# Gathered streams in a graph kernel: five loops of indirect DMAs that may not run more than a set number of columns ahead of their consumers

## The chip, the cores and the metric

The kernel runs on one core of a Trainium2 chip. A core has TensorE (PE), VectorE (DVE), ScalarE (ACT), GpSimd (POOL) and SyncE (SP), each with its own instruction stream; they meet through semaphores, and 16 DMA engines move data for them. The metric is the device time of one execution in microseconds (us), lower is better.

## The reference, cut to what matters

Four graph layers follow each other on 100000 nodes of 16 features and 50000 edges sorted by destination. Each layer normalizes the nodes, gathers a row of the source node for every edge, makes a message of it and sums the messages by destination:

```python
h = jnp.maximum(_layernorm(x, axis=-1), 0.0)
x = x + _L0_gnn_ref(h, edge_index, ...)   # attention, 3 heads, then 1 head: h[src] * alpha, twice
h = jnp.maximum(_layernorm(x, axis=-1), 0.0)
x = x + _L1_gnn_ref(h, edge_index, edge_type_8, ...)   # two passes: x[src] @ W[relation], mean by relation
h = jnp.maximum(_layernorm(x, axis=-1), 0.0)
x = x + _L2_gnn_ref(h, src, dst, edge_weight)          # messages summed at the source
h = jnp.maximum(_layernorm(x, axis=-1), 0.0)
x = x + _L3_gnn_ref(h, edge_attr_16, ..., src, dst, edge_type_90)   # h[src] @ W_rel[type] * e
```

## The kernel before

**Layout.** The edges are laid out as 128 partitions by T = 392 columns. A column of a gather is one indirect DMA that GpSimd issues: 128 rows of a table in DRAM, one to each partition, at indices from `src_i` or `idx2`. The program runs in stages; all engines meet at a barrier between two stages (L131, L132). In each stage every engine has one instruction stream, written out by the loops of its block, and the code's order is the order on the engine.

**The five gather streams that the change touches**, in the order of the program:

| stage | gathers (line before) | columns | consumer, unit | the use that is counted |
|---|---|---|---|---|
| first, attention layer 1 (`g1`) | `ring<-t_gat,src_i` L1147 | 56 to 391 (EARLY = 56 are gathered a section earlier) | VectorE, 48 columns, reads at L1271 | `mix_ok`, by `g_mix` L1362 |
| second, attention layer 2 (`g2`) | `g_ring<-t_gat,idx` L1487 | 0 to 391 | VectorE, 40 columns, L1617 | `ring_free`, by `g_S` L1637 |
| third, relation pass 1 (`r1`) | `r_ring<-t_rel,idx` L1817 | 0 to 391 | VectorE, 8 columns, L2010 | `expand_ok`, by L2010 |
| fourth, relation pass 2 (`r2`) | `r_ring<-t_rel,idx` L2128 | 0 to 391 | TensorE, 8 columns, L2160 | before `lift_ok` (L2160); in the change `taken`, after VectorE's reduce L2243 |
| last, layer 4 (`l3`) | `l_ring<-t_last,idx` L2573 | 0 to 391 | VectorE, 8 columns, L2655 | `mats_used`, after L2660 |

**What paces them.** A batch is eight columns with a landing semaphore `gat_in[n]` of its own. `paced` (L61 to L67) is asked before every gather; at each eighth column it waits for a landing: below column 160 (RUN) for that of the batch before the last, from 160 on for that of the batch just issued:

```python
    n = s // BATCH - (1 if s >= RUN else 2)
    if s % BATCH == 0 and n >= first // BATCH:
        engine.wait_ge(landing[n], 16 * BATCH)
```

`hold` is a plain `wait_ge`. In the second stage it keeps GpSimd from writing over a ring of 200 columns (NR = 5 blocks of QN = 40) that is still in use, at columns 200, 240, 280, 320 and 360; in the fourth, with 240 columns, at 240, 280, 320 and 360. In the third the ring has all columns and the hold is never reached. The consumers wait for their columns' landings with `all_landed` (L78 to L81).

After the gathers of the last stage GpSimd writes the result by columns into `fin` (L2583, 393 indirect DMAs, waits of `spaced` on L75 and of `final_ok`), and SyncE copies `fin` to the output. Two other streams of indirect DMAs stay as they are: the payload gathers of the first section (L521, landing waits on L520) and the scatter-adds between the fourth and the last stage (L2352, waits on L2351).

Of the kernel before, what the change touches and what calls it, by code (L numbers as in the profile page):

```python
# [69 lines left out]
def spaced(engine, landing, s):  # L70


    n = s // BATCH - 2
    if n >= 0:
        engine.wait_ge(landing[n], 16 * BATCH)  # L75


# [10 lines left out]
def gnn_kernel(nc, x, src, dst, edge_attr_16, edge_type_8, edge_type_90, edge_weight,  # L88
# [45 lines left out]
    with ExitStack() as top:  # L134
# [954 lines left out]
        with ExitStack() as ctx:  # L1089
# [52 lines left out]
            with nc.Block() as block:  # L1142
                @block.gpsimd
                def _(pool):
                    for s in range(EARLY, T):
                        paced(pool, gat_in, s, EARLY)
                        pool.indirect_dma_start(ring1[:, s, :], None, t_gat1,  # L1147
                                                bass.IndirectOffsetOnAxis(src_i[:, s:s + 1], 0)
                                                ).then_inc(gat_in[s // BATCH], 16)
                    all_landed(pool, gat_in, EARLY, T)  # L1150
# [270 lines left out]
        with ExitStack() as ctx:  # L1421
# [58 lines left out]
            with nc.Block() as block:  # L1480
                @block.gpsimd
                def _(pool):
                    for s in range(T):
                        if s % QN == 0 and s >= NR * QN:
                            hold(pool, ring_free, s // QN - NR + 1)
                        paced(pool, gat_in, s)
                        pool.indirect_dma_start(ring[:, s % (NR * QN), :], None, t_gat2,  # L1487
                                                bass.IndirectOffsetOnAxis(idx2[:, s:s + 1], 0)
                                                ).then_inc(gat_in[s // BATCH], 16)
# [272 lines left out]
        def relation_pass(tag, table, table_out, F, CW, weights, root, bias, NR, norm, setup):  # L1762
# [13 lines left out]
            with ExitStack() as ctx:  # L1776
# [32 lines left out]
                with nc.Block() as block:  # L1809
                    @block.gpsimd  # L1810
                    def _(pool):
                        for s in range(T):
                            if s % QN == 0 and s >= NR * QN:
                                i = s // QN - NR
                                hold(pool, expand_ok, first[i] + subs[i])
                            paced(pool, gat_in, s)
# [269 lines left out]
        with ExitStack() as ctx:  # L2086
# [33 lines left out]
            with nc.Block() as block:  # L2120
                @block.gpsimd
                def _(pool):
                    for s in range(T):
                        if s % QN == 0 and s >= NR * QN:
                            i = s // QN - NR
                            hold(pool, lift_ok, first[i] + subs[i])
                        paced(pool, gat_in, s)
# [411 lines left out]
        with ExitStack() as ctx:  # L2539
# [28 lines left out]
            with nc.Block() as block:  # L2568
                @block.gpsimd
                def _(pool):  # L2570
                    for s in range(T):
                        paced(pool, gat_in, s)
                        pool.indirect_dma_start(ring[:, s, :], None, t_last,  # L2573
# [133 lines left out]
```

## Time and profile before

| | us |
|---|---|
| median of 3 runs | 6640.55 |
| lowest, highest | 6635.97, 6644.13 |
| span of the profiled execution | 6645.3 |
| GpSimd busy in the span | 4320.0 (65%) |
| VectorE busy | 3659.5 (55%) |
| TensorE busy | 2965.9 (45%) |
| ScalarE busy | 1167.0 (18%) |

The profiled execution's time is 6645.3 us, of which its span is all, 4.8 us over the median of the runs. The rows below come from it. A row of a group of instructions gives their number, their busy time and mean duration, and the idle time of the engine just before them with what ended it; "issue" is idle time in which the engine waited for nothing that the profile shows. A landing wait shows as a wait for the DMA. EVENT_SEMAPHORE is an instruction that only waits for semaphores or sets them; POOLq is GpSimd's sequencer, which runs it. The chain of work that ended last consists of the writes to `fin` on GpSimd.

### The profile page before, as it was taken

How to read it: one execution, taken by the hardware profiler on the slowest of the kernel's cores; microseconds unless marked ns; L12 is line 12 of the kernel's file. 1: busy time of each engine (PE TensorE's matmuls, PEld its weight loads, DVE VectorE, ACT ScalarE, POOL GpSimd, SP SyncE). 2: the span in 40 equal slices, each digit the busy share in tenths (PEclk: the TensorE clock that was granted, in tenths of full speed). 3: DMA queues.
4: the chain of work that ended last, by engine and by line, in shares of the span. 5: the costliest groups of instructions: out<-in, count | busy, mean ns of one | idle time of the engine just before them, and what ended most of it. 6: DMA issues, size and time to landing. Idle time of an engine off the chain costs nothing. (4 is left out here: it accounts for less than half of the span.)

```text
span 6645.3 us, 44822 instructions
## 1 busy us (share of the span) xinstructions
PE 2965.9 (45%) x13056; PEld 2260.1 (34%) x13056; DVE 3659.5 (55%) x8917; ACT 1167.0 (18%) x1912; POOL 4320.0 (65%) x3949
## 2 busy tenths in 40 slices
PE   5798699974444344447655443111111002544000
PEld 2477555543333233346644333111111001433000
DVE  8855499976555566654347667433322068876000
ACT  0265454532222233211111100000000000000000
POOL 4666555557762776376657665888888823766776
PEclk9899899985666555556667665555555555776555
DMA  2122222221110322123222212222222234211001
GB/s 41 22 62 70 56 67 67 66 66 12 20 17 14 89 60 65 47 64 100 84 87 60 64 53 72 52 36 36 44 27 27 5 96 154 57 50 37 7 7 44
DMA packets 283354, 350.11 MB, mean 53 GB/s; under 512 B 133518, under 2 KB 204432, under 8 KB 281970
## 3 DMA queue, kind: packets, MB, share of 16 engines
q1 hardware_dynamic: 112158, 295.24, 13.2%
q0 software_dynamic: 169376, 41.40, 7.8%
q10 hardware_dynamic: 1576, 10.60, 0.7%
q8 instruction: 105, 1.72, 0.1%
q14 instruction: 139, 1.14, 0.1%
HBM read 231.06 MB, written 122.29 MB: 53 GB/s over the span
## 5 line engine op out<-in xcount | busy, mean ns | idle before, releaser
L2352 POOL DMA_INDIRECT acc<-l_rows,l_uniq x392 | 624.1, 1592 | 121.0 <-issue 108.6
L2573 POOL DMA_INDIRECT l_ring<-t_last,idx x392 | 392.4, 1001 | 366.5 <-ACTq L2568 207.6
L521 POOL DMA_INDIRECT pay<-in_x,gidx x392 | 460.1, 1174 | 235.4 <-DMA pay<-in_x,gidx 114.3
L2393 PE MATMUL ps_l<-l_msg,l_alike 128*128 128x16 f32 x784 | 176.3, 376 | 962.4 <-DVE l_msg L2456 962.4
L1487 POOL DMA_INDIRECT g_ring<-t_gat,idx x392 | 416.1, 1062 | 278.7 <-issue 110.1
L1817 POOL DMA_INDIRECT r_ring<-t_rel,idx x392 | 414.6, 1058 | 254.6 <-issue 110.3
L809 POOL DMA_INDIRECT t_sort<-pay,c_pos x392 | 384.8, 982 | 296.3 <-DVE c_pos L875 196.3
L901 PE MATMUL ps_c<-plane,c_hit 128*128 128x400 f32 x1568 | 542.6, 499 | 1.2 <-ACT c_hit L827 1.2
L2128 POOL DMA_INDIRECT r_ring<-t_rel,idx x392 | 392.7, 1002 | 224.4 <-issue 110.4
L2338 POOL DMA_INDIRECT l_ring<-t_mix,idx x392 | 426.3, 1087 | 154.6 <-issue 119.1
L2393 PEld LDWEIGHTS ps_l<-l_msg,l_alike 128*128 128x128 f32 x784 | 171.0, 331 | 967.7 <-DVE l_msg L2456 967.7
L1147 POOL DMA_INDIRECT ring<-t_gat,src_i x336 | 368.5, 1097 | 151.5 <-issue 93.3
L2583 POOL DMA_INDIRECT fin<-X,home_i x393 | 376.9, 959 | 119.8 <-issue 119.8
L2614 PE MATMUL ps_l<-w_rel,l_pick 128*128 128x256 f32 x784 | 275.7, 528 | 272.7 <-DVE l_pick L2643 272.7
L901 PEld LDWEIGHTS ps_c<-plane,c_hit 128*128 128x128 f32 x1568 | 296.4, 190 | 208.3 <-ACT c_hit L827 1.6
L2614 PEld LDWEIGHTS ps_l<-w_rel,l_pick 128*128 128x128 f32 x784 | 212.0, 277 | 336.1 <-DVE l_pick L2643 291.6
L2451 DVE TENSOR_SCALAR l_den<-l_ring 128x128 f32<-128x128 f32 x49 | 11.2, 228 | 564.3 <-DMA l_ring<-t_mix,idx 564.3
L871 DVE SCALAR_TENSOR_TENSOR c_junk<-iota_lo,lo_f,ps_c 128x400 f32<-128x400 f16 x392 | 231.0, 623 | 63.1 <-PE ps_c L901 63.0
L688 PE MATMUL ps_a<-w_ext,a_act_t 96*128 96x128 f32 x1600 | 224.5, 286 | 40.4 <-DVE a_row L612 39.9
L688 PEld LDWEIGHTS ps_a<-w_ext,a_act_t 96*128 96x128 f32 x1600 | 214.8, 200 | 61.7 <-DVE a_row L612 49.8
L1520 PE MATMUL ps_g<-ident,g_ex 128*128 128x128 f32 x300 | 71.9, 426 | 327.0 <-DVE g_ex L1704 327.0
L622 DVE SCALAR_TENSOR_TENSOR a_act_t<-a_ex,a_pos 96x512 f32<-96x512 f32 x200 | 137.4, 687 | 143.5 <-ACT a_ex L729 140.1
(529 smaller groups left out, 8145.0 us busy)
## 6 DMA issues: line engine op xcount, KB each, us to landing
c_rows_d<-row_dst SPq DMA_DIRECT2D x98, 256.0 KB, 3.3
l_keys<-row_at SPq DMA_DIRECT2D x49, 512.0 KB, 4.2
l_typs<-row_typ SPq DMA_DIRECT2D x49, 512.0 KB, 3.7
g_hs<-t_gat SPq DMA_DIRECT2D x30, 660.0 KB, 4.7
acc<-r_zero SPq DMA_DIRECT2D x60, 320.0 KB
t_rel<-r_row SPq DMA_DIRECT2D x30, 640.0 KB, 3.5
r_hs<-t_rel SPq DMA_DIRECT2D x30, 640.0 KB, 4.7
d_gain<-acc SPq DMA_DIRECT2D x30, 640.0 KB, 6.0
```

The costliest lines, as they stand in the source:

```text
L521: pool.indirect_dma_start(pay[:, s, 8:PAY], None, x, bass.IndirectOffsetOnAxis(gidx[:, s:s + 1], 0)).then_inc(gat_in[s // BATCH], 16)
L688: last = mm(ps[:, at:at + WIDE], act_t[:, u, P * m:P * (m + 1)], w2_ext[:], start=True, stop=True, skip_group_check=True)
L809: pool.indirect_dma_start(t_sort, bass.IndirectOffsetOnAxis(pos[:, e:e + 1], 0), pay[:, e, :], None).then_inc(sent, 16)
L901: last = mm(ps[:, bank:bank + LO], hit[:, b, j, P * s:P * (s + 1)], plane[:, b, LO * j:LO * (j + 1)], start=(j == 0), stop=(j == 1))
L1487: pool.indirect_dma_start(ring[:, s % (NR * QN), :], None, t_gat2, bass.IndirectOffsetOnAxis(idx2[:, s:s + 1], 0)).then_inc(gat_in[s // BA ...
L1817: pool.indirect_dma_start(ring[:, s % (NR * QN), :], None, table, bass.IndirectOffsetOnAxis(idx2[:, s:s + 1], 0)).then_inc(gat_in[s // BAT ...
L2128: pool.indirect_dma_start(ring[:, s % (NR * QN), :], None, t_rel2, bass.IndirectOffsetOnAxis(idx2[:, s:s + 1], 0)).then_inc(gat_in[s // BA ...
L2338: pool.indirect_dma_start(ring[:, s, :], None, t_mix, bass.IndirectOffsetOnAxis(idx2[:, s:s + 1], 0)).then_inc(gat_in[s // BATCH], 16)
L2352: pool.indirect_dma_start(acc[r], bass.IndirectOffsetOnAxis(uniq[:, s:s + 1], 0), rows[:, (s // ES) % RR, s % ES, :], None, compute_op=ALU.add
L2573: pool.indirect_dma_start(ring[:, s, :], None, t_last, bass.IndirectOffsetOnAxis(idx2[:, s:s + 1], 0)).then_inc(gat_in[s // BATCH], 16)
L2583: pool.indirect_dma_start(fin, bass.IndirectOffsetOnAxis(home_i[:, s:s + 1], 0), X[:, s, :], None).then_inc(sent[s // BATCH], 16)
L2614: last = mm(ps[:, at:at + 256], pick[:, e % 2, s], w_rel[:].rearrange("p i o -> p (i o)"), start=True, stop=True)
```

## The change

A helper `credit` is added and called before `paced` in the five gather loops; the two kinds of `hold` go. At every eighth column past `lead` it waits until the consumers have reported the use of all but the last `lead` columns: `lead` is 96 (2 * EW), 64, 64, 32 and 40. In the fourth stage the count is now `taken`, which VectorE raises after its reduce, in place of `lift_ok`.

```diff
--- before.py
+++ after.py
@@ -73,6 +73,12 @@
     n = s // BATCH - 2
     if n >= 0:
         engine.wait_ge(landing[n], 16 * BATCH)
+
+
+def credit(engine, used, s, lead, per):
+
+    if s % BATCH == 0 and s > lead:
+        engine.wait_ge(used, -(-(s - lead) // per))
 
 
 def all_landed(engine, landing, lo, hi):
@@ -1143,6 +1149,7 @@
                 @block.gpsimd
                 def _(pool):
                     for s in range(EARLY, T):
+                        credit(pool, mix_ok, s, 2 * EW, EW)
                         paced(pool, gat_in, s, EARLY)
                         pool.indirect_dma_start(ring1[:, s, :], None, t_gat1,
                                                 bass.IndirectOffsetOnAxis(src_i[:, s:s + 1], 0)
@@ -1481,8 +1488,7 @@
                 @block.gpsimd
                 def _(pool):
                     for s in range(T):
-                        if s % QN == 0 and s >= NR * QN:
-                            hold(pool, ring_free, s // QN - NR + 1)
+                        credit(pool, ring_free, s, 64, QN)
                         paced(pool, gat_in, s)
                         pool.indirect_dma_start(ring[:, s % (NR * QN), :], None, t_gat2,
                                                 bass.IndirectOffsetOnAxis(idx2[:, s:s + 1], 0)
@@ -1810,9 +1816,7 @@
                     @block.gpsimd
                     def _(pool):
                         for s in range(T):
-                            if s % QN == 0 and s >= NR * QN:
-                                i = s // QN - NR
-                                hold(pool, expand_ok, first[i] + subs[i])
+                            credit(pool, expand_ok, s, 64, ES)
                             paced(pool, gat_in, s)
                             pool.indirect_dma_start(ring[:, s % (NR * QN), :], None, table,
                                                     bass.IndirectOffsetOnAxis(idx2[:, s:s + 1], 0)
@@ -2121,9 +2125,7 @@
                 @block.gpsimd
                 def _(pool):
                     for s in range(T):
-                        if s % QN == 0 and s >= NR * QN:
-                            i = s // QN - NR
-                            hold(pool, lift_ok, first[i] + subs[i])
+                        credit(pool, taken, s, 32, ES)
                         paced(pool, gat_in, s)
                         pool.indirect_dma_start(ring[:, s % (NR * QN), :], None, t_rel2,
                                                 bass.IndirectOffsetOnAxis(idx2[:, s:s + 1], 0)
@@ -2569,6 +2571,7 @@
                 @block.gpsimd
                 def _(pool):
                     for s in range(T):
+                        credit(pool, mats_used, s, 40, ES)
                         paced(pool, gat_in, s)
                         pool.indirect_dma_start(ring[:, s, :], None, t_last,
                                                 bass.IndirectOffsetOnAxis(idx2[:, s:s + 1], 0)
```

GpSimd's instructions stand in the same order in both kernels, and those of the other engines are unchanged. What differs is the waits. In the rows below a name in brackets is a semaphore that the DMA, or an instruction just ahead of it, waits for. Semaphores are used again from stage to stage and are printed by the first name that each had: every name but the last one of a pair (`a_down`, `a_row2`, `s_rows` and so on) is the landing semaphore of an earlier batch of this stage.

GpSimd in the second stage, columns 184 to 200, before:

```order
L1487 DMA g_ring<-t_gat,idx 128x33 [waits a_down]
L1487 DMA g_ring<-t_gat,idx 128x33 x7
L1487 DMA g_ring<-t_gat,idx 128x33 [waits a_row2]
L1487 DMA g_ring<-t_gat,idx 128x33 x7
L1487 DMA g_ring<-t_gat,idx 128x33 [waits a_out2_0,g2_ring_free]
```

and with the change:

```order
L1493 DMA g_ring<-t_gat,idx 128x33 [waits a_down,g2_ring_free]
L1493 DMA g_ring<-t_gat,idx 128x33 x7
L1493 DMA g_ring<-t_gat,idx 128x33 [waits a_row2,g2_ring_free]
L1493 DMA g_ring<-t_gat,idx 128x33 x7
L1493 DMA g_ring<-t_gat,idx 128x33 [waits a_out2_0,g2_ring_free]
```

Column 200 has its two waits in both; columns 184 and 192, and every eighth column from 72 on, have a second one only now.

GpSimd at the end of the last stage's gathers, columns 376 to 391, and the first writes to `fin`, before:

```order
L2573 DMA l_ring<-t_last,idx 128x16 [waits a_gat_in20]
L2573 DMA l_ring<-t_last,idx 128x16 x7
L2573 DMA l_ring<-t_last,idx 128x16 [waits a_gat_in21]
L2573 DMA l_ring<-t_last,idx 128x16 x7
L2583 DMA fin<-X,home_i 152704x16 [waits a_gat_in32,a_gat_in34]
L2583 DMA fin<-X,home_i 152704x16 x15
```

and with the change (`a_gat_in29` stands for `mats_used`):

```order
L2576 DMA l_ring<-t_last,idx 128x16 [waits a_gat_in20,a_gat_in29]
L2576 DMA l_ring<-t_last,idx 128x16 x7
L2576 DMA l_ring<-t_last,idx 128x16 [waits a_gat_in21,a_gat_in29]
L2576 DMA l_ring<-t_last,idx 128x16 x7
L2586 DMA fin<-X,home_i 152704x16 [waits a_gat_in32,a_gat_in34]
L2586 DMA fin<-X,home_i 152704x16 x15
```

The gathers have a second wait from column 48 on; the writes to `fin` have what they had.

## Rows read from the trace of the kernel before

**Rows 1.** Groups by line, GpSimd: xcount | busy, mean ns | idle before <-releasers

```profile
L1147 POOL DMA_INDIRECT ring<-t_gat,src_i x336 | 368.5, 1097 | 151.5 <-issue 93.3 <-DMA ring<-t_gat,src_i 50.4 <-POOLq L132 7.8
L1487 POOL DMA_INDIRECT g_ring<-t_gat,idx x392 | 416.1, 1062 | 278.7 <-issue 110.1 <-POOLq L132 109.3 <-DMA g_ring<-t_gat,idx 59.3
L1817 POOL DMA_INDIRECT r_ring<-t_rel,idx x392 | 414.6, 1058 | 254.6 <-issue 110.3 <-POOLq L132 76.2 <-DMA r_ring<-t_rel,idx 68.1
L2128 POOL DMA_INDIRECT r_ring<-t_rel,idx x392 | 392.7, 1002 | 224.4 <-issue 110.4 <-DMA r_ring<-t_rel,idx 71.3 <-POOLq L132 34.4
L2573 POOL DMA_INDIRECT l_ring<-t_last,idx x392 | 392.4, 1001 | 366.5 <-ACTq L2568 207.6 <-issue 110.0 <-DMA l_ring<-t_last,idx 48.9
```

**Rows 2.** Waits of the consumers for gathers: us in total, times, longest us

```profile
DVE idx L1271 <- DMA ring<-t_gat,src_i: 71.5, 7, 13.9
DVE g_score L1617 <- DMA g_ring<-t_gat,idx: 108.6, 10, 35.7
DVE r_msg L2010 <- DMA r_ring<-t_rel,idx: 58.0, 7, 9.7
PE r_ps L2160 <- DMA r_ring<-t_rel,idx: 284.1, 49, 9.3
DVE l_pick L2643 <- DMA l_ring<-t_last,idx: 98.3, 32, 4.1
```

**Rows 3.** Timeline, stage ends: start us, us, engine line op [idle before <-releaser]

```profile
2047.54 0.21 DVE L1271 CAST idx<-ring 128x48 int32<-128x48 f32 x1 [12.76 <-DMA ring<-t_gat,src_i]
...
2753.66 0.21 DVE L1617 TENSOR_TENSOR g_score<-g_ring,g_ad_slot 128x32 f32<-128x32 f32 x1 [0.61 <-DMA g_ring<-t_gat,idx]
...
3410.62 1.23 DVE L2010 TENSOR_TENSOR r_msg<-r_ring,r_hot 128x1024 f32<-128x1024 f32 x1 [8.56 <-DMA r_ring<-t_rel,idx]
...
4041.33 0.48 PE L2160 MATMUL r_ps<-ident,r_ring 128*128 128x128 f32 x1 [3.62 <-DMA r_ring<-t_rel,idx]
...
6123.73 0.98 POOL L2583 DMA_INDIRECT fin<-X,home_i  x1 [0.30 <-issue]
```

**Rows 4.** Instructions up to a credit: count, ns min/median/max, first and last start us

```profile
L1487 POOL DMA_INDIRECT g_ring<-t_gat,idx x153: 938/944/2504, 2166.7 to 2377.6; - x153
L1637 DVE TENSOR_TENSOR g_S<-g_ring,ps_g x3: 1486/1486/1486, 2225.6 to 2347.0; 128x1280 f32<-128x1280 f32 x3
L2128 POOL DMA_INDIRECT r_ring<-t_rel,idx x49: 940/944/1274, 3455.8 to 3515.7; - x49
L2243 DVE TENSOR_REDUCE r_Y<-r_chosen x4: 1004/1006/1007, 3470.8 to 3489.9; 128x64 f32<-128x512 f32 x4
```

**Rows 5.** Semaphore instructions by line: count, ns min/median/max, first and last start us

```profile
L67 POOLq EVENT_SEMAPHORE  x9: 17/17/17, 2450.8 to 3988.2; - x9
L520 POOLq EVENT_SEMAPHORE  x35: 17/17/17, 82.8 to 739.2; - x35
L75 POOLq EVENT_SEMAPHORE  x10: 17/17/17, 6165.6 to 6610.0; - x10
L2351 POOLq EVENT_SEMAPHORE  x48: 42/43/43, 4220.0 to 5349.3; - x48
```

**Rows 6.** Timeline, second stage, GpSimd: columns 192, 200, 312 and 320

```profile
2439.47 0.94 POOL L1487 DMA_INDIRECT g_ring<-t_gat,idx  x1 [1.75 <-DMA g_ring<-t_gat,idx]
...
2451.54 0.94 POOL L1487 DMA_INDIRECT g_ring<-t_gat,idx  x1 [2.21 <-DMA g_ring<-t_gat,idx]
...
2626.70 0.94 POOL L1487 DMA_INDIRECT g_ring<-t_gat,idx  x1 [1.76 <-DMA g_ring<-t_gat,idx]
...
2638.71 0.95 POOL L1487 DMA_INDIRECT g_ring<-t_gat,idx  x1 [2.15 <-DMA g_ring<-t_gat,idx]
```

**Rows 7.** Timeline, first section, GpSimd: two landing waits of L521

```profile
253.57 1.50 POOL L521 DMA_INDIRECT pay<-in_x,gidx  x1 [2.19 <-DMA pay<-in_x,gidx]
...
282.07 2.42 POOL L521 DMA_INDIRECT pay<-in_x,gidx  x1 [1.69 <-DMA pay<-in_x,gidx]
```

**Rows 8.** GpSimd before the writes to fin: us in total, times, longest us

```profile
POOL fin L2583 <- issue: 119.8, 393, 0.3
```

## The prediction

> **What bounds the kernel now.** First the list of GpSimd's groups [rows 1]. Five stages that the change touches gather 336 to 392 columns each (one indirect DMA per column, 128 rows), and they look alike: a gather is busy for about 1.0 to 1.1 us, 0.3 us of "issue" lies before each, and once in eight, from column 160 on, the engine waits for its own landings. Per stage that is 25 to 30 such waits of 49 to 71 us in all [rows 1]. (The fourth's other four are the ones with the old hold.) Busy, issue and landing waits of the second stage are 416.1 + 110.1 + 59.3 = 585.5 us, and from its first gather's start, 2166.7, to its last one's end, 2751.3 + 0.9, pass 585.5 us. So GpSimd does nothing else and never waits for a consumer.
>
> Next, who waits for the gathers [rows 2]: the consumers do, in every stage: VectorE 10 times in the second, 7 times in the first and third, 32 times in the last; TensorE 49 times in the fourth. The last such waits stand at the end of their stages [rows 3]: column 336 of the first is awaited for 12.76 us, column 360 of the second for 0.61, column 376 of the third for 8.56, column 384 of the fourth for 3.62. In the last stage the column writes to `fin` follow the last gather on the same engine after 0.30 us, and the program's end is GpSimd's chain of these writes. Every one of the five gather streams therefore sets its stage's end: what a batch of eight costs more, the program pays.
>
> **Part 1, the credits as waits.** The credit holds a gather until the consumers have used all but 96, 64, 64, 32 or 40 columns. Would it ever hold? I laid each of the 203 credits against the use that it asks for. The smallest reserve is in the fourth stage, with its lead of 32: column 48, the 49th gather, starts at 3515.7, and its credit asks for the fourth reduce, L2243, which ends at 3489.9 + 1.0 = 3490.9, 25 us earlier. In the second stage it is column 152, the 153rd gather, at 2377.6; the third `g_S` product ends at 2347.0 + 1.5 = 2348.5, 29 us earlier [rows 4]. The other three stages have no less. The consumers wait for gathers, so they are never 32 to 96 columns behind. The credits hold nothing, no gather starts later by them, and nothing is gained from pacing: **0 us**. The same shows that the two old holds, at nine places, held nothing, so that taking them away gives no time either.
>
> **Part 2, the credits as instructions.** An instruction on GpSimd carries one wait of its own kind; a second one goes into a semaphore instruction ahead of it. The built order shows it: in the kernel before, the gathers of these stages have one wait each but for nine (five in the second stage, four in the fourth, where the old hold stood); in the changed one, 36 + 40 + 40 + 44 + 43 = 203 have two. So 194 semaphore instructions come in, and it is the landing wait that moves into them, since the credit, asked first in the code, stays on the DMA. The trace has these nine, all on L67 [rows 5]. Their own duration is 17 ns. What the move costs is seen from the gather after:
>
> With a semaphore instruction, column 200 starts after 2.21 us of idle time, column 320 after 2.15; without, columns 192 and 312, the batches before, after 1.75 and 1.76 [rows 6]. The differences are 0.46 and 0.39 us. The semaphore instruction of column 200 stands at 2450.8 [rows 5], when the landing is seen, and the gather starts at 2451.54, 0.7 us later. The payload gathers of the first section, L521, tell the same: of their 48 landing waits 35 stand on an instruction of their own [rows 5], for instance the one of 2.19 us, and 13 on the DMA, as the one of 1.69 [rows 7]: 0.50 apart. Behind the semaphore instruction on GpSimd are queued the gather itself and the seven of its batch, all of them later by this much. I take **0.48 us** for a landing wait that the engine really sits out, between the 0.46 of column 200 and the 0.50 of L521, where both kinds are many. The ends are the smallest difference, 0.39, and 2.21 - 1.69 = 0.52, across the two streams.
>
> [...]
>
> Where the landing came long before, the instruction is free. Below column 160 `paced` asks for the batch before the last. The 10 semaphore instructions on L75, for the writes to `fin`, are of that kind, and all 393 writes start 0.3 us after the one before [rows 5, 8]. So 58 of the 203 credits, those below column 160 (7, 11, 11, 15 and 14), cost 0.
>
> From column 160 on there are 29 landing waits per stage. In the first the one of column 384 comes after the last gather that anyone waits for, so 28; in the second 29 - 5 = 24 and in the fourth 29 - 4 = 25 are new; the third and the last have 29 each. Sum: 28 + 24 + 29 + 25 + 29 = 135, times 0.48 = **65 us**. By stage 13.4, 11.5, 13.9, 12.0 and 13.9. Nothing hides it: the engines that could are waiting for these very landings [rows 2, 3]. In the third stage VectorE has the columns up to about 264 in hand before it needs them, but the sum of the delays arrives at columns 272 to 376, where it waits. The second is bound by least, 0.61 us, yet VectorE is in it because of nine earlier waits of the same kind, 108.6 us with it [rows 2], and they slip too.
>
> The section with the scatter-adds and those before it keep their order and their time. So the profiled span goes from 6645.3 to 6645.3 + 65 = 6710. The median of the runs shown, 6640.55, is 4.8 us less than that span; against it the sum is 6640.55 + 65 = **6705 us**.
>
> **A term that I don't take.** Gathers last 1.00 to 1.10 us on average where the shortest and the median are 0.94 (the median stands in [rows 4]): over the 1904 gathers of [rows 1], busy for 1984.3 us, 1984.3 - 1904 x 0.944 = 187 us of stretch, in some of them, while VectorE and the other engines work. Spread over 3% more time it might shrink by as much, 6 us; or not. I keep it for the low end.
>
> **The rivals.**
> Costs more than it pays: mine, at 6705.
> (a) Not slower: the semaphore instruction costs only itself. All 194 at 17 to 43 ns [rows 5] are 3 to 8 us, which gives 6644 to 6649, within 0.2%. For it speaks that every instruction on L75 is hidden; against it, that the nine of exactly the kind in question are not. It decides at whether the landing is already there when the sequencer arrives: from column 160 on it is not. A page of the Trainium skill would price it so too (Advanced Engine Details and Errata, Network/Comms): reading a semaphore from a sequencer takes 50 to 100 ns, by which 135 would be an estimated 7 to 14 us; the nine rows of this trace say more.
> (b) Only the last stage pays, because the others find slack behind their last gathers: 6640.55 + 29 x 0.48 = 6654. Against it stand the waits of [rows 3].
> (c) The credits do hold. In the fourth stage the reserve is 25 us; if consumers that start late by 12 us lost that reserve (they would have to fall behind the gathers, not with them), each of the stage's ten slots could add some 1 to 3 us: 6715 to 6735.
> (d) Faster: gathers spread thinner leave VectorE undisturbed and the stretch of 187 us falls by 65 + 13 us, some 40%. As the distance between gathers and consumers does not change, I see nothing that would do it: 6627.
>
> **How the numbers follow.** Mine has 0.86, (a) 0.06, (b) 0.03, (c) 0.03, (d) 0.02. Mine alone spans 135 x 0.39 = 53 to 135 x 0.52 = 70 us: 6693 to 6711. Less the 6 us of stretch it begins at 6687, taken as 6686; landings in the third and fourth stage that collide otherwise than before (their landing waits vary most, 68.1 and 71.3 us in all [rows 1]) may add 7 us at the other end: 6718. That range, 6686 to 6718, holds about 0.8 of the chance; (a), (b) and (d) stay outside. 0.2% is 13 us, about what a measurement of this kernel can tell from no change. Faster by more: 0.02; within: (a) and half of (b), 0.07; slower by more: 0.91.
>
> **What would show it.** Right: 203 semaphore instructions on the landing wait's line in the changed trace; from column 160 on landing waits of 2.1 to 2.2 us where 1.6 to 1.8 stood, and each stage's gather stream longer by 11.5 to 14; the gathers below column 160 at 0.30 us as before; no wait of GpSimd put down to VectorE or to the credit. The third and the fifth stage begin 25 and 51 us later than before. Wrong would be: unchanged landing waits (then a), GpSimd waiting for `g_mix`, `r_Y` or `l_wide` (then c), a mean gather under 1.0 us (then d), or longer streams with stage ends that don't move (then b).

## The result, and the profile after

The changed kernel takes **6687.57 us** (median of 4 runs, 6681.19 to 6690.97) beside 6642.34 us for the kernel before on the same chip: ratio 1.007, 95% interval 1.0056 to 1.0085. It is 45 us slower; 65 were forecast, and the time lies 1.6 us above the low end of the range (6686). Its profiled span is 6679.1 us beside 6645.3. The two medians are 45 us apart and the two profiled spans 34, because the profile of before is one of its slower executions and the profile of after one of its faster ones; stage by stage I compare profiles, the total by medians.

That is one chip. Chips are not alike for this program: the experiments ran in three groups, each on one chip with the kernel before beside it, which took 6641.03, 7803.52 and 7782.79 us in them. On the last of these chips the same changed kernel was **10.8% faster** than before (below). The prediction speaks of the chip that its profile came from.

GpSimd's groups by line in the changed kernel, as in [rows 1] (xcount | busy, mean ns | idle before, releasers):

```profile
L1154 POOL DMA_INDIRECT ring<-t_gat,src_i x336 | 370.0, 1101 | 164.1 <-issue 91.4 <-DMA ring<-t_gat,src_i 58.2 <-POOLq L138 7.8
L1493 POOL DMA_INDIRECT g_ring<-t_gat,idx x392 | 416.7, 1063 | 288.4 <-POOLq L138 108.8 <-issue 107.9 <-DMA g_ring<-t_gat,idx 62.2
L1821 POOL DMA_INDIRECT r_ring<-t_rel,idx x392 | 409.0, 1043 | 257.4 <-issue 107.0 <-POOLq L138 76.3 <-DMA r_ring<-t_rel,idx 74.2
L2130 POOL DMA_INDIRECT r_ring<-t_rel,idx x392 | 388.9, 992 | 241.9 <-issue 111.2 <-DMA r_ring<-t_rel,idx 95.1 <-POOLq L138 35.6
L2576 POOL DMA_INDIRECT l_ring<-t_last,idx x392 | 380.4, 970 | 380.3 <-ACTq L2570 207.5 <-issue 106.0 <-DMA l_ring<-t_last,idx 66.7
```

Against [rows 1] the idle time grew by 12.6, 9.7, 2.8, 17.5 and 13.8 us, in all 56.4, and the busy time changed by +1.5, +0.6, -5.6, -3.8 and -12.0, in all -19.3. The three largest releasers of a group stand in these lines. The list of all waits of GpSimd has two more, which are put down to VectorE, the sign by which a credit that holds was to be known (us in total, times, longest us):

```profile
POOL g_ring L1493 <- DVE g_S L1643: 9.5, 4, 2.9
...
POOL ring L1154 <- DVE g_mix L1369: 6.6, 3, 2.2
```

They are landing waits as long as their neighbours. The operation named merely ended at about the time of the landing; the one that the gather's credit asks for had ended at least 55 us before the gather started. I laid all 203 credits of the changed trace against the use that they ask for, as the prediction did for the trace before: the smallest reserve is 24.8 us, again at column 48 of the fourth stage (where a use is four columns). So on this chip no credit held GpSimd.

The semaphore instructions of L67, as [rows 5] has them (count, ns min/median/max, first and last start), and behind them columns 192, 200 and 312 of the second stage, as in [rows 6] (start us, us, [idle before]).

```profile
L67 POOLq EVENT_SEMAPHORE  x203: 17/17/17, 1602.0 to 6147.1; - x102
```

The timeline of those columns:

```profile
2455.12 0.95 POOL L1493 DMA_INDIRECT g_ring<-t_gat,idx  x1 [2.18 <-DMA g_ring<-t_gat,idx]
...
2467.02 0.95 POOL L1493 DMA_INDIRECT g_ring<-t_gat,idx  x1 [2.21 <-DMA g_ring<-t_gat,idx]
...
2647.82 1.35 POOL L1493 DMA_INDIRECT g_ring<-t_gat,idx  x1 [2.30 <-DMA g_ring<-t_gat,idx]
```

Nine became 203. Column 200, which had its semaphore instruction before, waits 2.21 us as it did; columns 192 and 312, which had none, went from 1.75 and 1.76 us to 2.18 and 2.30.

Who waits for the gathers (as [rows 2]: us in total, times, longest us):

```profile
DVE g_score L1623 <- DMA g_ring<-t_gat,idx: 119.0, 10, 34.8
DVE l_pick L2646 <- DMA l_ring<-t_last,idx: 99.5, 31, 4.1
DVE idx L1278 <- DMA ring<-t_gat,src_i: 83.2, 7, 15.8
DVE r_msg L2014 <- DMA r_ring<-t_rel,idx: 52.2, 6, 9.8
PE r_ps L2162 <- DMA r_ring<-t_rel,idx: 297.9, 49, 9.3
```

The last such waits of the stages, and between them the third stage's first gather, behind them the first write to `fin` (timeline, as [rows 3]):

```profile
2059.32 0.20 DVE L1278 CAST idx<-ring 128x48 int32<-128x48 f32 x1 [15.83 <-DMA ring<-t_gat,src_i]
...
2776.78 0.21 DVE L1623 TENSOR_TENSOR g_score<-g_ring,g_ad_slot 128x32 f32<-128x32 f32 x1 [0.72 <-DMA g_ring<-t_gat,idx]
...
2851.53 0.94 POOL L1821 DMA_INDIRECT r_ring<-t_rel,idx  x1 [76.28 <-POOLq L138]
...
3430.89 1.23 DVE L2014 TENSOR_TENSOR r_msg<-r_ring,r_hot 128x1024 f32<-128x1024 f32 x1 [9.75 <-DMA r_ring<-t_rel,idx]
...
4061.46 0.47 PE L2162 MATMUL r_ps<-ident,r_ring 128*128 128x128 f32 x1 [8.79 <-DMA r_ring<-t_rel,idx]
...
6157.86 0.99 POOL L2586 DMA_INDIRECT fin<-X,home_i  x1 [0.30 <-issue]
```

The same consumers wait as before, and longer, but for `r_msg` of the third stage, whose stream did not grow. The second stage's last awaited column comes 23.1 us later than in [rows 3] and the first write to `fin` 34.1 us later, so the program pays what the streams pay. The third stage begins at 2851.5, 23 us later (25 were forecast); the last at 5604.4 instead of 5572.1, 32 us later (51 were forecast). The shortfall lies in the third and the last stream: the fourth's 582.8 us became 595.2, as forecast, the third's 593.0 became 590.1 and the last's 551.3 became 553.2.

### The profile page after: what moved, and what is told of

Read it like the earlier page. It is cut to its first block and busy times, and to the rows that moved or that the text cites. A ratio compares the mean times of both kernels' runs of the same rounds, so it can differ in the third digit from the quotient of the medians.

```text
span 6679.1 us, 45016 instructions
## 1 busy us (share of the span) xinstructions
PE 2967.6 (44%) x13056; PEld 2261.4 (34%) x13056; DVE 3659.5 (55%) x8917; ACT 1168.3 (17%) x1912; POOL 4299.8 (64%) x3949
```

## The experiments

Stream lengths are from a stream's first gather's start to its last one's end. First four kernels on one chip (kernel before: 6641.03 us, 23 runs).

**1. The credit on the semaphore instruction, the landing wait on the DMA.** All five loops of the changed kernel, with two lines swapped:

```diff
-                        credit(pool, mix_ok, s, 2 * EW, EW)
                         paced(pool, gat_in, s, EARLY)
+                        credit(pool, mix_ok, s, 2 * EW, EW)
```

> The changed kernel with the two waits in the other order in the code (landing wait first, credit second), so that the landing wait stays on the gather itself and the credit goes into the semaphore instruction. All 203 credits are still asked. Theory A (the 45 us come from landing waits that stand on a semaphore instruction): the time of the kernel before, 6642 us, ratio 1.000; landing waits of the second stage back at 1.7 to 1.8 us from 2.2. Rival B (keeping GpSimd within 32 to 96 columns costs or moves something by itself): about that of the changed kernel, 6688, ratio 1.007.

Measured: 6628.27 us, ratio 0.9985 (0.9976 to 0.9993). The same 203 credits, the same 194 added instructions, now for the credit (count, ns min/median/max, first and last start), and the loss is gone:

```profile
L81 POOLq EVENT_SEMAPHORE  x203: 17/17/17, 1597.1 to 6077.2; - x102
```

L81 is the wait in `credit`. Beyond that, 13 us are gained. The nine old landing waits now stand on their DMAs too, which at 0.48 us each would be 4.3, but by the streams they are worth more: the second and fourth are 11.7 and 6.5 us shorter than before (table below; 9.3 and 6.3 in experiment 3, where only those nine differ in them). The second stage shows how. Before, column 200's gather starts at 2451.54 [rows 6] and column 216's here:

```profile
2477.91 1.54 POOL L1487 DMA_INDIRECT g_ring<-t_gat,idx  x1 [1.76 <-DMA g_ring<-t_gat,idx]
```

In experiment 1 the same two:

```profile
2451.67 0.94 POOL L1493 DMA_INDIRECT g_ring<-t_gat,idx  x1 [1.77 <-DMA g_ring<-t_gat,idx]
...
2475.99 0.94 POOL L1493 DMA_INDIRECT g_ring<-t_gat,idx  x1 [1.73 <-DMA g_ring<-t_gat,idx]
```

The landing wait of column 200 is 0.44 us shorter, and behind it the sixteen gathers take 24.32 us where they took 26.37. The waits between them are alike; the gathers last less, since three of them took over 2 us before and one does now. So a batch that starts 0.44 us later can also bring its gathers to places where they last longer, and this one wait was worth 2.5 us. So neither the credits as waits nor the instructions' own time cost anything that can be seen here; rival (a)'s "costs only itself" is true of an instruction whose wait is met, and only of that.

**2. The second wait alone.** The kernel before, its old holds kept, with a wait for a landing two batches older than the one that `paced` asks for from column 160 on, met long before, at the places of the credits:

```diff
+def older(engine, landing, s, lead):
+    n = s // BATCH - 3
+    if s % BATCH == 0 and s > lead:
+        engine.wait_ge(landing[n], 16 * BATCH)
...
+                        older(pool, gat_in, s, 64)
```

> The kernel before, no credits, old holds kept; at the 203 places of the credits a second wait, for a batch's landing two batches older than the one that is awaited, which is always long past. Theory A: the semaphore instruction alone does it, 6688 us, ratio 1.007, landing waits of the second stage 2.2 us, gather streams of 526, 596, 590, 595 and 553 us as in the changed kernel. Rival B: 6642, ratio 1.000.

Measured: 6686.7 us, ratio 1.0076 (1.0059 to 1.0092). No consumer is asked, and the time is that of the changed kernel, stage by stage (table). The loss comes from the landing wait's place; the credits are not needed for it.

**3. The landing wait first everywhere.** The kernel before without any credit, the landing wait written ahead of the other wait in the second and fourth stage and in the first section (L521), where 35 payload gathers have two waits:

```diff
+                        if s >= BATCH and s % BATCH == 0:
+                            pool.wait_ge(gat_in[s // BATCH - 1], 16 * BATCH)
                         part, turn_no = divmod(s - 2 * NB, 6)
...
-                        if s >= BATCH and s % BATCH == 0:
-                            pool.wait_ge(gat_in[s // BATCH - 1], 16 * BATCH)
```

> The kernel before with the landing wait put first in the code at all 44 gathers that have a second wait: 35 payload gathers of the first section (L521), five in the second stage, four in the fourth. No credits. Theory A: each of these landing waits gets shorter by 0.4 to 0.5 us (2.2 to 1.7); the nine of the second and fourth stage give 4 us; the 35 give up to 17 more if the first section ends with its gathers: 6621, ratio 0.997. Rival (the first section is set by VectorE's and TensorE's work, for which GpSimd waits 25 us there, and the 17 us are lost in longer waits for it): 6638, ratio 0.9995.

Measured: **6612.56 us**, ratio 0.9961 (0.9946 to 0.9976), below both kernels, for the order of two lines. The first section's stream fell from 695.4 to 684.8 us. Of the 28 us gained 16 lie beyond experiment 1, 0.45 us for each of the first section's 35 waits.

**4. Credits in the third and the last stage alone**, where the changed profile shows the smallest gains in length:

```diff
-                            if s % QN == 0 and s >= NR * QN:
-                                i = s // QN - NR
-                                hold(pool, expand_ok, first[i] + subs[i])
+                            credit(pool, expand_ok, s, 64, ES)
...
+                        credit(pool, mats_used, s, 40, ES)
```

> Credits in the third and the last stage only, the other three as before. What it decides is why these two stages gave 3 us less and 2 us more where 13.9 more each were summed. Theory A1 (it belongs to these stages: in the last the first gather of a batch was held up by VectorE's pick operation in any case; in the third fewer landings are slow): third stream 590 us (before 593.0), last 553 (before 551.3), whole 6642. Rival A2 (in the third stage it was the phase in which the stage happened to begin, 23 us later than before): third stream 593 + 14 = 607, last 553, whole 6656. Rival A3 (the sum's full price): 607 and 565, whole 6670.

Measured: 6654.27 us, ratio 1.002 (1.0011 to 1.0029), 13 us above the kernel before for 58 landing waits, 0.23 us each. The two streams have the lengths of theory A1 (589.8 and 553.0 us), the time is near A2's 6656.

Stream lengths on chips of this kind, in us, by where the landing waits stand:

| stream | on the DMA: before, 1, 3 | on the semaphore instruction: after, 2, 4 |
|---|---|---|
| first | 512.2, 513.0, 511.3 | 526.3, 527.0 |
| second | (585.5), 573.8, 576.2 | 596.2, 594.6 |
| third | 593.0, 584.5, 585.4 | 590.1, 591.7, 589.8 |
| fourth | (582.8), 576.3, 576.5 | 595.2, 595.0 |
| last | 551.3, 550.9, 553.2 | 553.2, 552.1, 553.0 |

(In brackets: the kernel before has 5 and 4 of them on semaphore instructions. Experiment 4 leaves the first, second and fourth stage as before; they take 514.0, 586.3 and 581.2 us there.) Experiment 2 less experiment 1 is 14.0 + 20.8 + 7.2 + 18.7 + 1.2 = 61.9 us for 144 landing waits, 0.43 us each; their medians are 58.4 us apart. The average hides a wide spread: from about 0.5 us a wait in the first stream over 0.7 in the second and 0.6 in the fourth to 0.2 in the third and nearly nothing in the last. Two streams show little of it. For the third the kernel before was an unlucky witness: its 593.0 us hold eight landing waits of over 2.4 us, the other five traces five or six; against 584.5 and 585.4 the semaphore instructions cost 4 to 7 us there. The last is another matter. Its group by line in experiment 1:

```profile
L2576 POOL DMA_INDIRECT l_ring<-t_last,idx x392 | 391.9, 1000 | 366.3 <-ACTq L2570 207.4 <-issue 110.0 <-DMA l_ring<-t_last,idx 48.9
```

in experiment 3, the landing waits on the DMA as well:

```profile
L2573 POOL DMA_INDIRECT l_ring<-t_last,idx x392 | 394.3, 1006 | 366.4 <-ACTq L2568 207.5 <-issue 110.0 <-DMA l_ring<-t_last,idx 48.9
```

in experiment 2, on the semaphore instruction:

```profile
L2585 POOL DMA_INDIRECT l_ring<-t_last,idx x392 | 379.1, 967 | 380.5 <-ACTq L2579 207.5 <-issue 107.0 <-DMA l_ring<-t_last,idx 66.0
```

and in experiment 4, likewise:

```profile
L2578 POOL DMA_INDIRECT l_ring<-t_last,idx x392 | 379.9, 969 | 380.6 <-ACTq L2572 207.6 <-issue 107.0 <-DMA l_ring<-t_last,idx 66.1
```

The waits cost their 14 us (366.3 to 380.5), and the gathers themselves give 12 to 15 back (391.9 to 379.1). It is the first gather of each batch, which before lasts longer than the usual 0.944 us: at 23 of the 29 batches it starts during VectorE's pick, at the other six during the operation that writes `l_kept`. The timeline of the kernel before at one of them:

```profile
5934.82 0.75 DVE L2643 TENSOR_SCALAR l_pick<-l_typs,lane 128x1024 f32<-128x1024 f32 x1 [4.06 <-DMA l_ring<-t_last,idx]
5935.00 1.40 POOL L2573 DMA_INDIRECT l_ring<-t_last,idx  x1 [1.79 <-DMA l_ring<-t_last,idx]
```

and of the changed kernel:

```profile
5968.27 0.75 DVE L2646 TENSOR_SCALAR l_pick<-l_typs,lane 128x1024 f32<-128x1024 f32 x1 [3.97 <-DMA l_ring<-t_last,idx]
5968.92 0.94 POOL L2576 DMA_INDIRECT l_ring<-t_last,idx  x1 [2.16 <-DMA l_ring<-t_last,idx]
```

One landing releases VectorE's pick and GpSimd's next gather. Before, the gather starts 0.18 us into the pick of 0.75 us and lasts 1.40 us; after, it starts 0.65 us into it and lasts 0.94. From the pick's start to the gather's end pass 1.58 us and 1.59 us. The later start is what the gather had lost anyway. What lies above 0.944 us, summed over the stream's first gathers from column 160 on is 15.3, 15.3 and 15.6 us in the three traces with the wait on the DMA and 2.5, 2.5 and 2.2 in the three with it on the semaphore instruction. The Trainium skill has a rule that fits (SBUF - State Buffer, Who interferes with whom): VectorE, in a mode that uses both its ports, and GpSimd contend for one pair of them, and whoever starts first has it for the whole instruction. The trace agrees so far as the gather's end stays where it was; that it is this pair no run here shows.

That it is the pick the traces of experiments 5 and 6 (below) do show, though their times cannot be used for it. Experiment 5 has the landing wait on the DMA and the pick moved away: none of the 29 first gathers starts during a pick, and none lasts over 0.95 us; experiment 10 repeats it with the same result. In experiment 6 twenty gathers start 0.10 to 0.60 us into a pick. Two of them:

```profile
7028.07 0.75 DVE L2650 TENSOR_SCALAR l_pick<-l_typs,lane 128x1024 f32<-128x1024 f32 x1
7028.38 1.27 POOL L2580 DMA_INDIRECT l_ring<-t_last,idx  x1 [2.10 <-DMA l_ring<-t_last,idx]
...
7150.29 0.75 DVE L2650 TENSOR_SCALAR l_pick<-l_typs,lane 128x1024 f32<-128x1024 f32 x1
7150.79 1.07 POOL L2580 DMA_INDIRECT l_ring<-t_last,idx  x1 [2.29 <-issue]
```

The later the start, the shorter the gather: all twenty end 1.57 us after the pick's start. Two that start less than 0.10 us into a pick last 0.94 us. Not every VectorE operation does this: first gathers that start during `l_wide` or `l_mrow` last 0.94 or 0.95 us in experiments 5, 6 and 10.

**5 and 6. The pick taken away as cover.** Experiment 5 lets VectorE make its pick ahead of the landing wait, so that landing and pick part; experiment 6 adds the last stage's credits to it:

```diff
-                            all_landed(dve, gat_in, QN * i + ES * s, QN * i + ES * (s + 1))
...
+                            all_landed(dve, gat_in, QN * i + ES * s, QN * i + ES * (s + 1))
```

```diff
+                        credit(pool, mats_used, s, 40, ES)
```

> The kernel before, no credits; in the last stage VectorE does the pick operation L2643 (0.75 us, released by the same landing as GpSimd's next gather) ahead of the landing wait and no longer behind it. Theory A1 (that operation is what holds up the first gather of each batch, 15 us over the 29 batches from column 160 on): these gathers at 0.94 us, 15 us less in the last stream from this, 551 to some 537 us, unless the pick now holds up another gather; whole 6627 to 6641. Rival (the stretch has another cause): first gathers of a batch still at 1.4 us, stream 551. The first four streams are those of the kernel before and give a second look at them: theory of chance collisions in the third, 585 to 593 us; if they are a fixed consequence of the code, 593 again.

> e4_pick_early with the credits of the last stage added (landing wait on the semaphore instruction there), the other stages as before. Theory A1: the cover is gone, so the 29 waits cost their full price: last stream 29 x 0.48 = 13.9 us longer than that of e4_pick_early. Rival (something else in this stage absorbs them): about 2 us longer, as in the changed kernel against the one before.

Both ran on the chip on which the kernel before takes 7803.52 us. Measured: 7804.32 us, ratio 1.0017 (0.9973 to 1.006), and 7757.26 us, 0.9949 (0.9904 to 0.9993). What the waits cost without their cover these times cannot tell, since the last stage was paced by something else: with the credits GpSimd's last stream grew from 535.6 to 584.0 us and the writes to `fin` behind it shrank from 624.1 to 496.7.

**7 and 8. Less restraint, and more**, on that chip too (the kernel before: 7803.52 us, 19 runs). Experiment 7 lets every landing wait ask one batch further back; experiment 8 is experiment 1 with the shortest reach that can be met:

```diff
-RUN = 160
+RUN = T
```

```diff
-                        credit(pool, mix_ok, s, 2 * EW, EW)
+                        credit(pool, mix_ok, s, EW + 8, EW)
...
-                        credit(pool, ring_free, s, 64, QN)
+                        credit(pool, ring_free, s, QN + 8, QN)
...
-                            credit(pool, expand_ok, s, 64, ES)
+                            credit(pool, expand_ok, s, 16, ES)
```

(and 16 for 32 and for 40 in the last two).

> The kernel before with RUN = T, so that no gather waits for the batch just issued, only for the one before it. What it decides is whether a sat-out landing wait is paid in full by the program, as the prediction's sum took it. Theory A: the landing waits of the five streams (40 + 47 + 59 + 71 + 39 us over the 0.3 of issue, from column 160 on) go, the streams end earlier by most of that, and the time falls until another engine sets the stage ends: 6640 - 256 = 6385 at best, 6450 if VectorE and TensorE cap it. Rival C (the stage ends are set by the consumers' own work): hardly any change, 6600 to 6640. Rival D (more gathers in flight make landings and gathers slower): slower than 6640.

> e1_landing_first with the leads cut from 96, 64, 64, 32, 40 to 56, 48, 16, 16, 16 columns, so that credits do hold. Theory A with the reserves of the trace (25 to 33 us at the old leads, 1.3 us a column): a lead shorter by 40, 16, 48, 16 and 24 columns takes 52, 21, 62, 21 and 31 us of reserve, so all but the second and fourth would now be asked for too early: GpSimd waits for VectorE, up to 20 to 40 us once per 48 columns in the first stage, whole 6700 to 6850. Rival (pacing helps the consumers, and a tight lead helps more): below 6628.

Measured: 7956.96 us, ratio 1.0222 (1.0137 to 1.0307), and **7030.53 us, 0.9047** (0.8968 to 0.9125). In kind experiment 7 went as theory D had it and experiment 8 as the rival, though both were priced for a chip of the first kind. The further ahead GpSimd may run on this chip, the slower the program; held back, it gives 10% back. On a chip of the first kind neither was run, so what a looser or tighter reach does there is not known.

**9 to 12. The change itself on such a chip.** The third group ran on a third chip, where the kernel before takes 7782.79 us. Experiment 9 is the changed kernel, 10 and 11 repeat 5 and 6, and 12 is experiment 8 with the landing wait first in the first section too (the edit of experiment 3).

> The changed kernel itself, beside the others of this group. On a chip where the kernel before takes about 6640 us: ratio 1.007 again, the fifth stream 552 to 555 us. On a chip where it takes about 7800 us the theories differ. Theory A (the credits reach back 64 columns and more, the consumers on that chip fall behind by more than that, so the credits hold GpSimd there): below the kernel before by some per cent, between 7100 and 7700 us, and the semaphore instructions' 45 us vanish in it; credits show up as waits of GpSimd for VectorE. Theory B (the reaches are too long to bite there either): 7800 to 7850 us, GpSimd again waiting 200 us and more at the barriers behind its streams.

> The kernel before with VectorE's pick of the last stage put ahead of its wait for the landing, no credits. Where the kernel before takes about 6640 us, theory A (in the fifth stream the later start of a batch's first gather was hidden by the pick, which started with it on the same landing and made it 1.4 us long instead of 0.94): the fifth stream shrinks by 10 to 13 us, from 551 to 538 to 541, and the total falls to about 6629 us. Theory B (the pick has nothing to do with the gather's length): the stream stays at 551 and the total at 6640. Where it takes about 7800 us: within 0.5 per cent of it.

> The same with the credits of the last stage alone, as the change has them. Where the kernel before takes about 6640 us, theory A: the fifth stream is 11 to 14 us longer than in the kernel without these credits, 550 to 554 us, since no pick is left that covers the semaphore instruction. Theory B (something else covered it): it stays within 3 us of the kernel without them. Where it takes about 7800 us: shorter than the kernel without them by 40 to 80 us, in the stage behind the fifth stream.

> All five credits at their shortest reach that can be met (56, 48, 16, 16, 16 columns) and every landing wait first in the code, that of the first section too. Where the kernel before takes about 6640 us, theory A (the five reserves of 25 to 33 us stay behind GpSimd, so that even a shorter reach seldom bites): 6610 to 6630 us. Theory B (credits of 16 columns bite, since a use is signalled for 8 or 16 columns at once): each stream longer by 10 to 60 us, 6680 to 6800 us in all. Where it takes about 7800 us: 7000 to 7030 us, as the same credits gave without the edit in the first section.

Measured: experiment 9 **6944.75 us, ratio 0.8921** (0.8859 to 0.8982); 10 7762.82 us, 0.9951 (0.9916 to 0.9985); 11 7706.85 us, 0.9909 (0.9866 to 0.9952); 12 7014.39 us, 0.9016 (0.8971 to 0.9062). My theory A for experiment 9 held in kind, but the time is far below the 7100 to 7700 that I gave it.

There is no trace of the kernel before on such a chip; experiment 10, within 0.5% of it, stands for it. GpSimd's waits in experiment 10 (us in total, times, longest us), those for the barriers and for VectorE:

```profile
POOL r_ring L2128 <- POOLq L132: 488.1, 1, 488.1
POOL g_ring L1487 <- POOLq L132: 346.9, 1, 346.9
POOL r_ring L1817 <- POOLq L132: 248.4, 1, 248.4
POOL l_ring L2338 <- POOLq L132: 231.4, 1, 231.4
...
POOL fin L2583 <- DVE X L2672: 113.1, 6, 46.1
```

L132 is the barrier between stages. GpSimd finishes its stream and then waits 231 to 488 us for the consumers; [rows 1] has 109.3, 76.2 and 34.4 there. The picture of the first section of the prediction, consumers waiting for GpSimd, is turned round. The same view of the changed kernel on the same chip, experiment 9:

```profile
POOL g_ring L1493 <- POOLq L138: 108.4, 1, 108.4
...
POOL r_ring L1821 <- POOLq L138: 76.4, 1, 76.4
POOL r_ring L1821 <- DVE r_msg L2014: 71.0, 9, 23.2
...
POOL ring L1154 <- DVE g_mix L1369: 57.2, 3, 53.0
...
POOL r_ring L2130 <- DVEq L2247: 54.3, 8, 17.6
...
POOL r_ring L2130 <- POOLq L138: 42.5, 1, 42.5
POOL g_ring L1493 <- DVE g_S L1643: 39.7, 5, 30.6
...
POOL l_ring L2576 <- DVEq L2666: 30.9, 5, 11.3
```

These are 3 + 5 + 9 + 8 + 5 = 30 waits of 57.2 + 39.7 + 71.0 + 54.3 + 30.9 = 253 us. Nine of them are landing waits of 2.1 to 2.4 us put down to VectorE, as in the trace on the first chip: the use that their credit asks for lay 19 us back or more. At the other 21 the gather starts 0.3 us after that use, so the credits hold 21 times, for 233 us, and for that the barrier waits of 347, 248 and 488 us are 108, 76 and 43 again, as on the first chip. The tight reaches of experiment 12 hold more in the first stage (7 waits of VectorE's `g_mix`, 207.9 us) and end 70 us later, with a first stream of 665.3 instead of 568.9 us: there the change's own reach is the better one. Of the other four streams two are longer by 5 and 11 us and two shorter by 4 and 8; since experiment 12 also has the landing waits first, its reaches are not judged apart from that. For the last stage's credits alone experiments 10 and 11 say the same in small: stream and writes to `fin` 535.5 + 620.1 us without, 587.4 + 509.7 with them, 58 us less.

What makes the consumers slow while GpSimd runs free? The timeline of one place of the third stage in experiment 10, GpSimd's lines left out:

```profile
3381.36 1.92 PE L1876 MATMUL r_ps<-rel_w,r_msg_t 128*128 128x32 f32 x8 [9.28 <-issue]
...
3425.53 0.37 ACT L1954 COPY r_Y<-r_ps 128x256 f32<-128x256 f32 x1 [44.21 <-DMA pay<-in_x,gidx]
```

ScalarE copies what TensorE has just multiplied. The product ends at 3383.3 and the copy starts at 3425.5, 42.25 us later. By the kernel's code it waits for this product alone. The releaser that the row names, a payload gather finished long ago, cannot be it; and the only DMA packets of these 42 us are those of GpSimd's queue, so the trace shows no transfer of instruction code there. Of the 49 such copies (L1954) six start while the third stage's gather stream runs (3250.7 to 3789.9), and all six are late, by 36 to 42 us, 247 us in sum; none of the 43 behind it is. The stage is 400 us longer here than in the trace of before, from its first gather to the next stage's. The same 42.25 us came in experiments 5, 6, 7 and 11, on both chips. In experiment 9, whose credits hold GpSimd in this stage, 47 copies start during the stream, and two are more than 10 us late (35.8 and 12.9). In the six traces of the first kind of chip each starts 0.04 us after the product. So on these chips work of one engine for another can start late while GpSimd's stream runs; whether it is the semaphore that comes late or the waiting instruction that goes late, the traces do not tell. What delays it, and whether the semaphore instructions themselves help there beside the held credits, stays open: experiments 1 and 2 were not run on such a chip.

## Why the prediction was right, and where its size was off

**Who sets the end**: right on the first chip. The streams, and nothing behind them, carry the loss; the consumers' waits grew with them, the third's apart.

**The credits as waits, 0 us**: right there (experiment 1). The argument "consumers wait for gathers, so they are never that far behind" holds only as far as its premise, and on chips of the other kind the premise is false: 21 holds. Its sign, "no wait of GpSimd put down to VectorE", was too blunt: the changed trace has seven such waits, all of them landing waits; the reserves, 24.8 us and more, say that nothing held. I took the reserves of 25 and 29 us [rows 4] for a property of the program; they are one of the chip.

**The landing wait on the semaphore instruction**: right, and settled from both sides: the loss goes when the wait goes back to the DMA (1) and comes without any credit (2). The count of 203 is as forecast; the wait of most columns is 2.1 to 2.3 instead of 1.6 to 1.8.

**0.48 us each, 65 us**: the mis-sized term. That 45 us still lies in the range is luck in part: it begins at 6686 only by the 6 us of "a term that I don't take", the main sum alone began at 6693, and 6687.57 is below that. By medians (the kernel before is within 1.3 us in both groups) the changed kernel stands 59 us above experiment 1 where 144 x 0.48 = 69 would, and the kernel before 13 us above it where its nine would give 4.3. So of the 20 us missing 10 are at the one end and 8 at the other. The price of one wait was right: from the landing to the next gather's start pass 0.26 us in the median where the wait is on the DMA and 0.74 where it is on the semaphore instruction, in the first, second and last stream of all six traces. What it does to its stream was not: as the gathers behind it start later, they last longer in one stage and less long in another. The 8 are the nine old waits, worth 1.4 us apiece by the medians and about 2 by their streams (experiment 1), so that the kernel before had more of the loss in it already than nine times 0.48. By profiles, idle time and busy time apart:

| stream | forecast | idle | busy |
|---|---|---|---|
| first | 13.4 | +12.6 | +1.5 |
| second | 11.5 | +9.7 | +0.6 |
| third | 13.9 | +2.8 | -5.6 |
| fourth | 12.0 | +17.5 | -3.8 |
| last | 13.9 | +13.8 | -12.0 |

The waits alone are near the sum, 56 of 65; the third's part is mis-sized since landings in the profile of before happened to be slow there. What I had wrong is one price for all stages, and "Nothing hides it". I looked for cover only among engines that wait for the landing, and found none; the cover was a collision that the later start avoids. **"A term that I don't take"**, 6 us for the low end, is that term: it is 19 us by the two profiles, and not spread thin but 12 of it in one place, the first gather of each batch beside VectorE's pick or `l_kept`. Had I looked at the 29 gathers behind the landing waits apart in the trace of before, the 1.40 us of 23 of them beside the usual 0.94 would have shown that 0.46 of the 0.48 us were already being paid in the last stage. The working would have been 65 - 13 = 52.

**The rivals.** (a) falls by experiments 1 and 2 together; (b) had the right sign and the wrong stage: the last one pays least; (c) falls on this chip and is what happens on the others, with the opposite sign of its price; (d), fewer collisions, is real as a part of the sum, and its sign, a mean gather under 1.0 us, stands in two stages (992 and 970 ns).

## What to carry to other kernels

Where an instruction has two waits, write first the one that it will really sit out: the first stays on the instruction, and a later one goes to a semaphore instruction ahead of it, which cost 0.43 us a time on average here, between nearly nothing in one stage and over 2 us at single places, as the gathers behind it fell. Two lines in the right order gave 28 us (experiment 3), and gave the credits for nothing (experiment 1). Before pricing a later start, look whether the instruction starts into a collision: its end may not move. And a bound on how far one engine may run ahead cannot be judged by one chip's reserves: the same change lost 0.7% on one, all of it by the order of two waits, and gained 10.8% on another, where the bound itself holds.

## What the hardware showed that I had not expected

The same program takes 6641 us on one chip and 7783 and 7804 us on two others, at a granted TensorE clock of 0.65 and 0.63 in their profiles. The difference is not in the engines' work: VectorE is busy 3659.5 us in experiment 1 and 3657.6 in experiment 5, GpSimd 4309.3 and 4216.4, TensorE 2976.3 and 2975.8. It is in waits between engines, some of which end 42.25 us after their cause while GpSimd's gather stream runs; the traces were followed at one place of one stage, and what else adds to the difference stays open.

A gather's busy time is no constant of 0.94 us: started 0.18 us into a VectorE pick of 0.75 us it lasts 1.40, started 0.30 into it 1.27, 0.50 into it 1.07, 0.65 into it 0.94. The end is what stays, 1.57 us after the pick's start up to a start at 0.60.
